# A four-layer transformer pass in fp32 by split operands: the order of work in the turns of its second half, and at the seam between its halves

## The reference

```
x = x + latent_attention(ctx, layernorm(x))   # 8 heads of 128; keys and values from [layernorm(ctx), latents]
x = x + ffn(layernorm(x))                     # gelu(x W1' + b1) W2' + b2, 1024 hidden
                                              # W1' = W1 + scale * m1, W2' = W2 + scale * m2, per batch:
                                              # m1, m2 are outer products of rows 1..16 of the layer's input
x = x + attention(layernorm(x), ctx)          # one head of 256
x = x + experts(layernorm(x))                 # 8 experts silu(x Wg) * (x Wu) -> Wd, mixed by routing weights
                                              # made of sigmoid(x Wr): exps, a zone test, a top-2 fallback, a division
```

## Time and profile before

| | |
|---|---|
| time, median of 3 runs | 1973.57 us (1971.06 to 1973.63) |
| the profiled execution | 1971.35 us, its span 1969.4 us |
| mean granted TensorE clock | 0.996 |
| PE busy | 1906.7 us, 97% of the span, 13822 matmuls |
| DVE busy | 1468.5 us, 75% |
| ACT busy | 1215.5 us, 62% |
| POOL busy | 393.2 us, 20% |
| DMA | 119.24 MB, mean 61 GB/s |

### The profile page before, as it was taken

One profiled execution on the slowest core, in us unless ns is written; L12 is line 12 of the kernel. 1 busy time (PEld: TensorE's weight loads), 2 busy tenths in 40 slices (PEclk: granted clock), 3 DMA queues, 4 the chain that ended last, 5 costly groups with the idle time before them and its releaser, 6 DMA issues.

```text
span 1969.4 us, 41605 instructions
## 1 busy us (share of the span) xinstructions
PE 1906.7 (97%) x13822; PEld 1772.8 (90%) x13822; DVE 1468.5 (75%) x3616; ACT 1215.5 (62%) x2538; POOL 393.2 (20%) x614
## 2 busy tenths in 40 slices
PE   7999999999999999999997999999999999999998
PEld 6888888888889888888887999999999999999998
DVE  7877777777876776777756677787877777787775
ACT  5656566555655565555674666766776667666753
POOL 2222222222222222222435101111111111111100
PEclk9999999999999999999998999999999999999999
DMA  3021012201110000000325633343332333333300
GB/s 121 28 71 63 17 59 69 69 11 66 62 53 22 11 11 21 21 11 11 69 71 164 209 81 60 73 82 75 62 82 63 79 68 70 77 76 61 83 7 12
DMA packets 101974, 119.24 MB, mean 61 GB/s; under 512 B 39072, under 2 KB 87072, under 8 KB 101920
## 3 DMA queue, kind: packets, MB, share of 16 engines
q1 hardware_dynamic: 93216, 83.93, 14.2%
q0 software_dynamic: 8704, 34.61, 9.8%
HBM read 97.29 MB, written 21.23 MB: 60 GB/s over the span
## 4 chain that ended last, share of the span: by engine, by line
PE 62%; DVE 11%; ACT 11%; issue 7%; DMA 6%; DVEq 1%; POOL 0%; ACTq 0%; SPq 0%; POOLq 0%
PE ring L648 9%; PE ring L650 9%; PE ring L649 9%; DMA b_x_s<-x_between 6%; PE ring L701 4%; PE ring L1903 4%; PE ring L1905 4%; PE ring L1904 4%; PE sim L648 3%; PE sim L650 2%; PE sim L649 2%; DVE b_act_e L1536 2%; PE ps_x L648 2%; PE ps_x L649 1%; PE ps_x L650 1%
## 5 line engine op out<-in xcount | busy, mean ns | idle before, releaser
L433 ACT ACTIVATE a_pr<-sim,a_nmax 128x512 f32<-128x512 f32 x256 | 174.4, 689 | 212.2 <-DVE a_nmax L563 212.2
L1903 PE MATMUL ring<-b_xch,b_weh 128*128 128x256 f32 x1024 | 291.5, 285 | 0.0
L1905 PE MATMUL ring<-b_xch,b_wel 128*128 128x256 f32 x1024 | 286.6, 280 | 0.0
L1904 PE MATMUL ring<-b_xcl,b_weh 128*128 128x256 f32 x1024 | 286.6, 280 | 0.0
L344 POOL TENSOR_SCALAR a_pr<-a_pr,a_rinv 128x512 f32<-128x512 f32 x256 | 183.7, 734 | 448.7 <-DVE a_rinv L573 445.9
L1262 ACT ACTIVATE b_heh<-b_act_e 128x512 fp32r<-128x512 f32 x128 | 80.9, 632 | 226.2 <-DVE b_act_e L1536 224.0
L1904 PEld LDWEIGHTS ring<-b_xcl,b_weh 128*128 128x128 f32 x1024 | 193.8, 189 | 0.0
L1903 PEld LDWEIGHTS ring<-b_xch,b_weh 128*128 128x128 f32 x1024 | 192.9, 188 | 0.0
L1905 PEld LDWEIGHTS ring<-b_xch,b_wel 128*128 128x128 f32 x1024 | 192.5, 188 | 0.0
L541 DVE SCALAR_TENSOR_TENSOR a_ktl<-ring,a_bkv_s,a_kth 128x512 fp32r<-128x512 f32 x128 | 95.3, 744 | 100.7 <-ACT a_kth L413 100.6
L554 DVE TENSOR_TENSOR a_ptl<-ring,a_pth 128x512 fp32r<-128x512 f32 x256 | 163.9, 681 | 7.3 <-ACT a_pth L423 6.2
(11 more groups left out here) (346 smaller groups left out, 6350.2 us busy)
## 6 DMA issues: line engine op xcount, KB each, us to landing
b_w2l_raw<-in_W2T POOLq DMA_DIRECT2D x16, 1088.0 KB, 8.7
b_even_b<-rows_between SPq DMA_DIRECT2D x16, 1024.0 KB, 5.5
b_w1l_raw<-in_W1T POOLq DMA_DIRECT2D x16, 1024.0 KB, 9.3
b_w1l_raw<-in_We SPq DMA_DIRECT2D x8, 768.0 KB, 4.5
expert_halves<-b_w1h SPq DMA_DIRECT2D x8, 768.0 KB, 3.3
expert_halves<-b_w1l SPq DMA_DIRECT2D x8, 768.0 KB, 5.6
b_weh<-expert_halves SPq DMA_DIRECT2D x8, 768.0 KB, 10.0
b_wel<-expert_halves SPq DMA_DIRECT2D x8, 768.0 KB, 11.2
```

The costliest lines, as they stand in the source:

```text
L433: nc.scalar.activation(pr[:, h % 2, t, :], sim[t][:], ACT.Exp, bias=nmax[:, h % 2, t:t + 1], accum_out=rsum[:, h % 2, t:t + 1]).then_inc(e ...
L1903: nc.tensor.matmul(out, lh, rh, start=(n == 0), stop=False)
L1904: nc.tensor.matmul(out, lh, rl, start=False, stop=False)
L1905: last = nc.tensor.matmul(out, ll, rh, start=False, stop=(n == len(parts) - 1))
```

## The change

1. **Turns, DVE and PE.** `second_residual(t)` stands ahead of the routing's last three stages and last product instead of behind them; the statistics of x2 are split in two (`row_moments`, `moments_joined`) and stand between those stages. `transposed(t, "B")` moves ahead of down 2 on PE. `bias_x1` moves ahead of the routing. `hidden(i, 4)` moves ahead of the statistics of the next x1, `bias_x2` and `norm_apply(t+1, "A")` go behind the product `queries_low`, the latter behind `maxima`. At a turn's end `hidden(i, 7)` comes ahead of `norm_apply(t, "C")`, and `hidden_low(i, 6)` behind it. On POOL, `rstd_of(t, "B")` comes ahead of `weights_added(t+1, "1")`.
2. **Turns, ACT.** A gelu of one column from a constant (`gelu_first`) stands between `silu(i, 1)` and `hidden_high(i, 1)`, so that the gelu table's load stands there.
3. **Seam.** The chain of batch 0 is reordered: biases folded and x2 normalised earlier, V and Q made together after head 6's scores, `queries_high` ahead of head 6's exps, `o_fill(0)` ahead of head 6's product with the values. POOL's four `weight_low` go to DVE; its transfer for W2 goes behind head 7's probabilities. `w_piece` numbers W1's pieces the other way, so that pieces 0 and 1 hold all of hidden columns 0 to 511.
4. **Two parts of batch 1's first layer in the seam.** `h_fill(1, 0)` follows `("T", 7, 1)` and `h_fill(1, 1)` follows `("O", 7)`; turn 1 is written out and starts its `h_fill` at part 2. The loop covers 2 to 13. On SP, `rows_spread(2)` goes behind the last projection.

```diff
-        with eng.Fori(1, B - 2) as t:
+        body(1, True, True, True, SEAM_PARTS)
+        with eng.Fori(2, B - 2) as t:
             body(t, True, True, True)
...
             def turn(t, chain, more, more2, parts=0):        # ScalarE
                 i = t - 1
                 silu(i, 1)
+                if chain:
+                    nc.scalar.activation(gelu_first[:], mhalf[:, 0:1], ACT.Gelu)
                 hidden_high(i, 1)
                 if chain:
-                    gelu_high(t, 0)
...
+                    for n in range(parts, HC // 2):
+                        gelu_high(t, n)
...
-                routing(i, 2)                                 # VectorE
-                if chain:
-                    bias_x1(t)
-                routing(i, 3)
+                routing(i, 7, 11)
                 if chain:
                     second_residual(t)
-                    norm_stats(t, "B", x2_s)
+                routing(i, 11, 12)
+                if chain:
+                    dve.wait_ge(x2_ready, t + 1)
+                    row_moments(t, "B", x2_s)
+                routing(i, 12, 13)
+                if chain:
+                    moments_joined(t, "B")
+                routing(i, 13, ROUTE)
                 weigh(i, 0)
...
+                hidden(i, 4)
                 if more:
                     dve.wait_ge(x1_in, t * 16 + 32)
                     norm_stats(t + 1, "A", x1_s)
-                hidden(i, 4)
...
+                hidden(i, 7)
+                if chain:
+                    norm_apply(t, "C", x3_s)
                 hidden_low(i, 6)
-                if chain:
-                    norm_apply(t, "C", x3_s)
-                hidden(i, 7)
                 weigh(i, 5)
...
                     v_fill(t)                                 # TensorE
-                down(i, 2)
-                if chain:
                     pe.wait_ge(x2_ready, t + 1)
                     transposed(t, "B")
+                down(i, 2)
...
-            if (h, done) == (7, ("O", 6)):                    # TensorE, seam
+            if (h, done) == (7, "scores"):
                 o_fill(0)
+            if (h, done) == (7, ("T", 7, 1)):
+                pe.wait_ge(first.sems["exp_done"], B * E * ST)
+                pe.wait_ge(lo["A"], 2)
+                pe.wait_ge(w_lo["1"], 4 + 2)
+                h_fill(1, 0)
             if (h, done) == (8, ("O", 7)):
+                h_fill(1, 1)
                 pe.wait_ge(lo["O"], 1)
...
-            if (h, done) == (5, "exps"):                      # ScalarE, seam
+            if (h, done) == (5, "begin"):
                 copy_high(0, "V", hh[:, V, 0:S])
                 act.wait_ge(uv_step, 2)
                 queries_high(0)
```

More of the change, by code:

```diff
@@ L836, in ffn_attention_experts @@
     x3_s = put("low", "x3_s", [P, ST, D])
+    gelu_first = put("low", "gelu_first", [P, 1])
     ident, mhalf = first.ident, first.mhalf
@@ L1058, in rest, with turn @@
             sp.sem_inc(out_done, 16)
-            def turn(t, chain, more, more2):
+            def turn(t, chain, more, more2, parts=0):
                 if more2:
@@ L1197, in beside, with turn @@
                 rstd_of(0, "C")
-                for q in range(4):
-                    weight_low(1, "1", q)
+                weights_added(1, "2")
         def rest():
-            def turn(t, chain, more, more2):
+            def turn(t, chain, more, more2, parts=0):
                 if more:
                     odd_scaled(t + 1)
-                if more:
-                    weights_added(t + 1, "1")
                 if chain:
@@ L1368, in beside @@
                 softmax_exps(0)
[L1369 removed]
+            if (h, done) == (6, "exps"):
                 copy_high(0, "T", hh[:, PT, 0:S])
@@ L1651, in distances, with routing @@
                 .then_inc(dist_ready, 1)
-        def routing(i, part):
+        def routing(i, first_stage, last_stage):
             v = nc.vector
@@ L1805, in turn @@
                     weight_low(t, "2", 2)
+                    if parts == 0:
+                        gelu_low(t, 0)
                     weight_low(t, "2", 3)
-                    for n in range(HC // 2):
+                    for n in range(max(parts, 1), HC // 2):
                         gelu_low(t, n)
-                routing(i, 0)
+                    bias_x1(t)
+                routing(i, 0, 5)
                 hidden(i, 2)
-                routing(i, 1)
+                routing(i, 5, 7)
                 if chain:
@@ L2075, in beside @@
                 transposed(0, "B")
-            if (h, done) == (4, ("T", 4, 1)):
+            if (h, done) == (5, "scores"):
                 pe.wait_ge(wqkv_lo, 4)
@@ L2079, in beside @@
                 v_fill(0)
-            if (h, done) == (5, "scores"):
                 pe.wait_ge(lo["B"], 1)
```

96 lines of the change are left out of this document (54 added, 42 removed).

## The result

The changed kernel takes 1926.07 us (median of 4 runs, 1923.24 to 1927.89), the kernel before beside it 1972.72 (4 runs, 1971.06 to 1973.63): ratio 0.9763, 95% interval 0.9746 to 0.9780. That is 46.7 us faster. The profiled execution took 1926.72 us, 44.6 less than the 1971.35 of before.

A forecast was written before the change was run, and what follows sets the result against it. TensorE, busy 97% of the span, bounds the kernel; only its waits and half-clock time can be won. Seam 11.7 + turn 1 4.0 + turns 18.5 = 34.2 us from 1971.35: 1937.2, plus 2.2 for the median, rounded to 1940; range 1930 to 1955.

The forecast's parts named there:

- 8.9 without the moved parts: Seam: net gain of 11.7 us, less the 2.8 us of the two parts moved in from turn 1.
- The three products: Seam: `o_fill(0)`, `h_fill(1, 0)` and `h_fill(1, 1)`, 1.41 us each, fill TensorE's waits at heads 6, 7 and the projection.
- are the same work, done in waits: Seam: the two parts leaving turn 1 are already in the seam's 11.7 us, being done in waits.
- 4.0 + 2.8: Turn 1: 4.0 us from its 2.3 us wait and 1.7 of half clock, plus 2.8 of moved parts.
- The experts' transfers of the seam end ten us earlier than its x1 load, as before: Turn 1: the seam's expert transfers are over ten us ahead of the x1 load; turn 1's gain was 4.0 us.
- 18.5 for 32.9: Turns 2 to 15: predicted gain 18.5 us, from 17.6 + 5.4 = 23.0, less 3.1 for restarts, less 1.4.
- the larger term: Turns, `s_fill`'s wait for the low queries: it goes, worth 15.5 + 13 x 0.16 = 17.6 us.
- Now the residual stands ahead of the routing's end: Turns, `s_fill`: residual 2.9 us earlier, x1 load (8.4 us issue to use) lands about 1401.7, wait goes; 17.6 us.
- my bound for the two waits: Turns 2 to 15: 23.0 us, the 17.6 of `s_fill`'s wait plus the 5.4 of `y_fill`'s.
- Less one step of 0.12 at each of 26 former waits for the restart (3.1): Turns 2 to 15: a 3.1 us deduction from the 23.0 for restarting at the former waits.
- less 1.4: Turn's end, around `hidden_low(i, 6)` and down 6: a charge of 0.1 us a turn, 1.4 us in all.
- The rival that a switch costs more: ScalarE's gelu table load: overruns idle time by a further 1.3 us, so `y_fill`'s gain fails; 1944 us, chance 0.06.

The follow-up runs named there:

- the kernel without two of them: Changed kernel with all four parts of batch 1's first layer made in turn 1, none in the seam: 1925.39 us.
- expert 5 moved: Changed kernel with expert 5's two loads issued on SyncE between the writes and reads of the spread rows: 1921.42 us, repeated 1922.77 us.
- both orders put back: Changed kernel with the residual and its statistics again behind the routing's end, expert 4's hidden step behind x1's statistics: 1925.12 us, 53.67 a turn.
- the ladder: Kernel before plus, cumulatively, GpSimd's order (1959.41 us), early gelu (1947.84), gelu's low half first (1939.59), x1's bias ahead of the routing (1938.45).
- three things put back: Changed kernel with the residual's place, expert 4's hidden step and GpSimd's order (W1's transfer ahead of rstd B) as before: 1927.65 us, 53.61 a turn.

## Why the prediction was right or wrong

**The seam: right.** Predicted 8.9 without the moved parts, measured 8.8. The waits left from head 4's scores on sum to 4.9 us (the rows above less the 1.2 ahead of the seam, and three of 0.5, 0.3 and 0.2 that are not shown) where I had walked out 5.6, and the clock stayed up. The three products did fill waits, as the kernel without two of them shows. That the two parts "are the same work, done in waits" held.

**Turn 1: the size right, one condition wrong.** With expert 5 moved, turn 1 was 6.7 us shorter than before; I had 4.0 + 2.8. With the turns' orders alone it was 4.3 shorter, for my 4.0. In the changed kernel it was only 1.8. The step that failed here is "The experts' transfers of the seam end ten us earlier than its x1 load, as before". In the kernel before the last of them landed 4.9 us ahead of the load's issue, in the changed kernel 7.1 us behind it. I had seen that `rows_spread(2)` holds the experts' loads back and asked only when the experts are wanted, not what shares the DMA engines with them.

**Turns 2 to 15: direction right, size wrong (18.5 for 32.9), mechanism of the larger term wrong.** The step that failed is "Now the residual stands ahead of the routing's end ... the load's landing at about 1401.7 ... The wait goes". The residual and the load's issue did come 3.0 us earlier, as I had said, and the wait went; but with both orders put back it stayed away at a cost of 0.15 us a turn, so it does not hang on them. The load's duration, 8.4 us in my sum, was 2.6. The chain was named rightly (load, statistics, hidden step, low queries). What shortened it, by the ladder, were 0.59 us a turn from the transfer that no longer runs beside W1's, 0.84 from gelu's table, 0.53 from gelu's low half ahead of a weight's, 0.36 from x1's bias, 0.17 from the rest with the residual. I had given the second 0.39 and the first, third and fourth nothing. These shares hold for this order of the edits: taken from the changed kernel, the early gelu is worth 0.50. The residual's new place alone in the kernel before was not run, and there it might have taken some of the share of GpSimd's order, since it too puts the load's issue ahead of W1's, as the changed kernel with GpSimd's order put back shows. What is shown is that the other edits do without it. I read the residual's edit as the cause, since it was the one with a story, and did not put a price on small moves in front of the same chain. So 23.0 us, my bound for the two waits, was not all there was to win.

**The deductions.** "Less one step of 0.12 at each of 26 former waits for the restart (3.1)" and "less 1.4" were not there: 4.5 us of the missing 14.4. The first took the same step off twice, since the 0.42 and 1.23 us lost at the waits had already been counted less 0.12. Nor had I counted stops too short for the view of waits. In one turn of before, the first matmul of down 2 starts 0.25 us behind the last of `v_fill`, where 0.12 is a step,

```profile
1453.85 0.28 PE L1905 MATMUL ps_c<-b_wvh,b_ctl 128*128 128x256 f32 x1
1454.10 0.35 PE L1903 MATMUL ring<-b_weh,b_heh 128*128 128x256 f32 x1
1454.30 0.28 PE L1904 MATMUL ring<-b_wel,b_heh 128*128 128x256 f32 x1
```

and the next 0.20: 0.21 us lost, and no idle time shown. Adding up what lies beyond a step wherever two starts are more than 0.13 us apart, a turn of 4 to 13 loses 3.4 us before and 0.8 after; some 0.5 of the difference stands at such places.

**Table and clock.** The rival that a switch costs more was wrong (0.03 us around the load). Of the 2.6 us ahead of the seam, where the change does nothing, 1.7 are half clock, 3.4 us at half speed in before and none after. Both executions wait for GpSimd there, 1.9 and 1.8 us; before shows 0.66 in the window behind it, after 1.00:

```profile
966.60:971.60 5.00, 4.47 (x17) 3.68 (x18) 4.91 (x11) 2.07 (x5) 4.30 (x6) 0.66 0.19 55
```
```profile
966.00:971.00 5.00, 4.53 (x29) 3.81 (x27) 4.97 (x11) 1.98 (x4) 4.30 (x7) 1.00 0.18 56
```

The +1.5 at the end is the same, the other way: behind the last turn's wait of 2.8 us the clock is 0.66 over 5 us in after, and 1.00 in before. Such stretches come and go between executions.

**What stays open.** With three things put back, W1's packets began 2.7 to 2.9 us behind their issue, where in the kernel before it was 2.0; this let the load through, and nothing here shows why. In two other kernels with the changed kernel's queue turn 1's load came in time (7.4 and 7.6 us); in both the residual and W1's issue come later in the turn, and expert 7's last load landed 3.5 us behind W1's issue instead of 4.8. No run moved W1's issue in turn 1 alone. And the residual alone in the kernel before is the run that would say what it is worth by itself.

## What to carry to other kernels

When a wait hangs on a chain, list everything on the chain's engines between the last point that is early and the wait, transfers included, and price each edit by what it takes out of that; then look what is spare, since an edit behind that point buys only slack. Ask of a load's duration what else was in flight, and in how many packets: it belongs to the moment, not to the load. To find which of many edits counts, add them one by one to the old kernel; taking one away from the new kernel shows nothing where another gives slack. The share that an edit gets still depends on its place in the order.

## What the runs showed of the hardware

A 256 KB load from SyncE's queue took 8.3 to 8.8 us behind a 1024 KB accumulating transfer that GpSimd had issued 1 us earlier, and 2.5 to 2.8 us when it was first; the large one took 9.3 and 8.4. The Trainium skill (DMA: Bandwidth & Descriptors, Issuing engines are not separate DMA queues) says that they share the same 16 engines and interleave. The trace agrees. An equal sharing by bytes would by an estimate from these rows have cost the small load about its own 2.6 us more, not 6. The sharing seen is by packets: 196 of 4 KB and 190 of 1 KB in the same 4.5 us. With 256 packets each, both transfers are through at about the same time.
